# Local attention in a whole-model kernel: layer constants behind the late addition, output products apart, turned banks copied in another order

## What is computed

```python
def local_attn(x, Wqkv, Wout):          # 8 heads of 64, windows of 64 rows
    q, k, v = jnp.split(x @ Wqkv.T, 3, axis=-1)
    q, k, v = map(towin, (q, k, v))
    ke, ve = (expand(k), expand(v))      # window before, own, after
    sim = jnp.einsum('bhnid,bhnjd->bhnij', q, ke) * SCALE
    attn = jax.nn.softmax(where(valid, sim, -1e9), axis=-1)
    o = jnp.einsum('bhnij,bhnjd->bhnid', attn, ve)
    return merge_heads(o) @ Wout.T
```

## Time and profile before

| | us |
|---|---|
| median of the three runs | 2078.7 |
| lowest, highest | 2075.09, 2084.13 |
| the profiled execution | 2071.32 |
| its span | 2069.5 |

### The profile page before, as it was taken

How to read it: one execution, slowest core, us unless ns; L and a number is a source line. 1 busy time by engine, 2 the same in 40 slices (tenths; PEclk the granted TensorE clock), 3 DMA queues, 4 the chain that set the end, 5 groups by cost and what they waited for, 6 DMA issues and landing times. The chain is left out here.

```text
span 2069.5 us, 67244 instructions
## 1 busy us (share of the span) xinstructions
PE 1839.4 (89%) x27305; PEld 1286.0 (62%) x27305; DVE 1509.0 (73%) x3679; ACT 1518.7 (73%) x4403; POOL 509.2 (25%) x605
## 2 busy tenths in 40 slices
PE   3888888886899999999988995879999999997998
PEld 1444444443477777677767873537777777775786
DVE  6989999997377788877875654637667676786454
ACT  3889999995588887787754557858888888774454
POOL 2000000000144344344331100114444444433110
PEclk9989999998999999999998997989999999999999
DMA  6655555550000000000001000000000000001101
GB/s 190 151 131 122 122 130 121 124 129 1 11 18 18 23 13 23 13 23 13 23 13 42 1 1 1 1 11 13 23 21 15 23 13 23 19 17 27 48 27 37
DMA packets 72805, 91.87 MB, mean 44 GB/s; under 512 B 9913, under 2 KB 65598, under 8 KB 68702
## 3 DMA queue, kind: packets, MB, share of 16 engines
q1 hardware_dynamic: 71346, 87.14, 18.0%
q10 hardware_dynamic: 1152, 0.43, 0.1%
HBM read 39.67 MB, written 31.10 MB: 34 GB/s over the span
## 5 line engine op out<-in xcount | busy, mean ns | idle before, releaser
L448 ACT ACTIVATE r_pr<-r_dist,k_negc 128x512 f32<-128x512 f32 (+1 forms) x512 | 368.2, 836 | 17.6 <-PE r_dist L337 10.1
L1301 POOL TENSOR_TENSOR f1l_pn<-f1l_p,f1l_rs 128x512 f32<-128x512 f32 (+1 forms) x256 | 208.6, 836 | 313.1 <-DVE f1l_rs L1083 313.1
L1301 POOL TENSOR_TENSOR f2l_pn<-f2l_p,f2l_rs 128x512 f32<-128x512 f32 (+1 forms) x256 | 207.5, 831 | 301.8 <-DVE f2l_rs L1083 301.8
L996 ACT ACTIVATE f1l_p<-f1l_sm,f1l_nb 128x192 f32<-128x192 f32 x512 | 212.0, 434 | 55.7 <-DVE f1l_nb L1076 55.7
L996 ACT ACTIVATE f2l_p<-f2l_sm,f2l_nb 128x192 f32<-128x192 f32 x512 | 212.0, 434 | 45.2 <-DVE f2l_nb L1076 45.2
L351 PE MATMUL r_acc<-r_pr,r_vp 128*32 128x128 f32 (+2 forms) x3584 | 200.9, 337 | 30.7 <-DVE r_pr L537 19.2
L529 DVE SCALAR_TENSOR_TENSOR r_pr<-r_pr,k_lo,r_cap 128x512 f32<-128x512 f32 x256 | 179.9, 744 | 9.5 <-ACT r_pr L448 9.2
L537 DVE TENSOR_SCALAR r_pr<-r_pr,k_hi,k_lo 128x768 f32<-128x768 f32 x256 | 163.5, 675 | 4.6 <-ACT r_pr L448 2.6
L827 PE MATMUL f1l_pj<-f1l_xt,k_wqkv 128*128 128x512 f32 x244 | 133.4, 629 | 2.2 <-ACT f1l_qt L976 1.4
L827 PE MATMUL f2l_pj<-f2l_xt,k_wqkv 128*128 128x512 f32 x244 | 132.9, 627 | 2.4 <-ACT f2l_qt L976 1.4
L1076 DVE TENSOR_REDUCE f2l_nb<-f2l_sm 128x4 f32<-128x768 f32 x128 | 116.0, 947 | 16.8 <-PE f2l_sm L858 16.6
(11 more groups left out here) (418 smaller groups left out, 4725.2 us busy)
## 6 DMA issues: line engine op xcount, KB each, us to landing
rbf_rows<-r_part SPq DMA_DIRECT2D x112, 128.0 KB, 1.9
r_qs<-rbf_rows SPq DMA_DIRECT2D x30, 384.0 KB
r_ks<-rbf_rows SPq DMA_DIRECT2D x30, 384.0 KB
f1l_vs<-f1l_vv SPq DMA_DIRECT2D x64, 128.0 KB, 2.4
f2l_vs<-f2l_vv SPq DMA_DIRECT2D x64, 128.0 KB, 2.4
rbf_rows<-r_part SPq DMA_DIRECT2D x16, 384.0 KB, 2.6
rbf_rows<-r_part SPq DMA_DIRECT2D x16, 256.0 KB, 2.9
out<-k_x SPq DMA_DIRECT2D x16, 256.0 KB, 2.3
```

The source lines that it names most:

```text
L448: nc.scalar.activation(pr[:, n % RING, e, cols], dist[:, e, cols], ACT.Exp, scale=K["negc"][:, h:h + 1]).then_inc(done, 1)
L996: ins = nc.scalar.activation(p[:, u % 2, k, :], sm[:, u % 2, k // 2, k % 2 * PW:(k % 2 + 1) * PW], ACT.Exp, bias=nb[:, u % 2, k:k + 1], ac ...
L1301: ins = nc.gpsimd.tensor_tensor(pn[:, u % 2, at:at + HU * w].rearrange("p (k c) -> p k c", k=HU), p[:, u % 2, :, cols], r.broadcast_to([P, ...
```

## The change

On VectorE the constants move from behind `leave_turned(2t+1)` to behind `leave_values(2t-1)`; `route_shift` moves from there to behind the first `reciprocals`; and in even units the `tp` copy goes ahead of the tail's. On TensorE `turn` gets a wait for `s_ps` ahead of the transposes into `xa`; and in the 14 steps that end with `use(b+2, 0)` (`ahead`) the four output products are spread: one after the first turn, one after the second, two after the third projection. In all other steps they stay where they are.

```diff
--- before.py
+++ after.py
@@ -869,6 +869,7 @@
                 for k in range(HU):
                     nc.tensor.transpose(tp[:, k * P:(k + 1) * P], pn[:, u % 2, k * P:(k + 1) * P], K["ident"][:])
                 wait(pe, s_oe, n - n % 2)
+                wait(pe, s_ps, n)
                 for k in range(HU // 2):
                     mm = nc.tensor.transpose(xa[:, 0, XS + k * P:XS + (k + 1) * P],
                                              pn[:, u % 2, (HU + k) * P:(HU + k + 1) * P], K["ident"][:])
@@ -905,13 +906,15 @@
                                                   skip_group_check=True)
                 mm.then_inc(s_pv, 1)
 
-            def output(t, half):
-                if half == 0:
+            def output(t, chunks):
+                if t < 0:
+                    return
+                if chunks[0] == 0:
                     pe.wait_ge(s_oe, 2 * t + 2)
-                for c in (2 * half, 2 * half + 1):
+                for c in chunks:
                     mm = nc.tensor.matmul(xa[:, 1, XO:XO + P], ot[:, t % 2, c, :], K["wout_l"][:, c * P:(c + 1) * P],
                                           start=(c == 0), stop=(c == HP - 1))
-                if half == 1:
+                if chunks[-1] == HP - 1:
                     mm.then_inc(s_w, 1)
 
             for k in range(1 + 2 * HP):
@@ -928,19 +931,22 @@
             def step(t):
                 b, i = t // NT, t % NT
                 more = b + 1 < B
+                ahead = i == NT - 1 and b + 2 < B
                 if more:
                     use(b + 1, 3 * i + 1)
                 turn(2 * t)
-                if t:
-                    output(t - 1, 0)
+                output(t - 1, (0,) if ahead else (0, 1))
                 if more:
                     use(b + 1, 3 * i + 2)
-                if t:
-                    output(t - 1, 1)
+                if not ahead:
+                    output(t - 1, (2, 3))
                 turn(2 * t + 1)
+                if ahead:
+                    output(t - 1, (1,))
                 if more:
                     use(b + 1, 3 * i + 3)
-                if i == NT - 1 and b + 2 < B:
+                if ahead:
+                    output(t - 1, (2, 3))
                     use(b + 2, 0)
                 values(2 * t)
                 if t + 2 < T:
@@ -959,8 +965,7 @@
             for t in range(T):
                 step(t)
             places()
-            output(T - 1, 0)
-            output(T - 1, 1)
+            output(T - 1, (0, 1, 2, 3))
 
         @block.scalar
         def _(act):
@@ -1086,8 +1091,11 @@
                 b, par, u = place(n)
                 dve.wait_ge(s_t, n + 1)
                 wait(dve, s_pv, n - 1)
+                if u % 2 == 0:
+                    nc.vector.tensor_copy(pt[:, u % 2, 0:HU * P], tp[:]).then_inc(s_pt, 1)
                 nc.vector.tensor_copy(pt[:, u % 2, HU * P:], xa[:, 0, XS:XS + 2 * P]).then_inc(s_ps, 1)
-                nc.vector.tensor_copy(pt[:, u % 2, 0:HU * P], tp[:]).then_inc(s_pt, 1)
+                if u % 2 == 1:
+                    nc.vector.tensor_copy(pt[:, u % 2, 0:HU * P], tp[:]).then_inc(s_pt, 1)
 
             def leave_values(n):
                 b, par, u = place(n)
@@ -1250,22 +1258,6 @@
                     route_step(t - 1)
                 if t:
                     leave_values(2 * t - 1)
-                if t < NT * SEARCH:
-                    route_shift(t)
-                if finding:
-                    pick(first)
-                leave_turned(2 * t)
-                if soon:
-                    reciprocals(2 * t + 2)
-                if t:
-                    residual(t - 1)
-                if finding:
-                    pick(first + 1)
-                leave_turned(2 * t + 1)
-                if soon:
-                    reciprocals(2 * t + 3)
-                if finding:
-                    pick(first + 2)
                 k = 2 * (t - NT * ANGLES)
                 if C and NT * ANGLES <= t < NT * FRACTIONS and k < SINES:
                     constant(k)
@@ -1276,6 +1268,22 @@
                     constant(k)
                     if k + 1 < CONSTANTS:
                         constant(k + 1)
+                if finding:
+                    pick(first)
+                leave_turned(2 * t)
+                if soon:
+                    reciprocals(2 * t + 2)
+                if t < NT * SEARCH:
+                    route_shift(t)
+                if t:
+                    residual(t - 1)
+                if finding:
+                    pick(first + 1)
+                leave_turned(2 * t + 1)
+                if soon:
+                    reciprocals(2 * t + 3)
+                if finding:
+                    pick(first + 2)
                 leave_values(2 * t)
 
             for t in range(T):
```

## The result

| | before | after |
|---|---|---|
| median of six runs, us | 2077.15 | 2114.69 |
| lowest, highest | 2074.61, 2084.13 | 2107.32, 2116.55 |
| profiled execution, its span | 2071.32, 2069.5 | 2113.92, 2112.1 |

The changed kernel is slower by 1.85%: the ratio is 1.0185, 95% interval 1.0166 to 1.0203. Forecast were +29.9 us and 2108.6 us; the medians differ by 37.5 us and the two profiled spans by 42.6 us.

A forecast was written before the change was run, and what follows sets the result against it. TensorE was taken to bound the kernel, 89% busy. Terms +38.7 - 9.9 + 1.1 = +29.9 us on the profiled 2071.3 us gave 2101.2 us; plain runs lie 7.4 us higher, so 2108.6 us, range 2088 to 2123.

The forecast's parts named there:

- Part 1, the chain: Last steps of a batch: product, residual, copies and L824 become serial; L824 1.32 us later, 28 times, +38.7 us with search steps.
- The search steps: Steps 51 and 55 of each stage: `pick` between residual and copies adds an estimated 0.43 us each, 1.7 us in all.
- Part 2, the constants: First light stage, batches 4 to 9: constants moved to where POOL is idle regain most of 11.64 us, -9.9 us.
- the four steps that I had expected to stay long: Constants exceeding the room before the copy: the eight L1206 cost 0.7 us, steps 24, 36 and 38 0.2 to 0.4 each.
- Under 3 us: Sign that the forecast is right: batches 4 to 9 of the two light stages differ by less than 3 us.
- Part 3, the shift: `route_shift` behind the first reciprocal is blocked by POOL; mean 0.53 to about 1.3 us, 0.015 us in 72 steps, +1.1 us.
- The order: POOL starts 0.25 us after the first reciprocal, L1110 would start 0.26 us after it, so L1110 was taken as blocked.
- Part 4: Full copy first in even units, and TensorE's added wait for the tail's copy: cost 0, gain 0, bounds -2 and +2 us.
- The hole filled: Rival: copies of the second turn don't wait for products, the 0.42 us hole ahead of L824 goes; -21.7 us, 2057, chance 0.08.
- The boundary at a third of its cost: Rival: other PE work or a shorter chain absorbs part of the batch-end cost; +4 us, 2083 us, chance 0.06.
- constants whose excess stays: Rival: the constants' excess has another cause and stays, so the change does little; +39.8 us, 2118 us, chance 0.07.
- POOL's second instruction going first: Rival: L1110 also waits for the second of POOL's pair, another 0.57 us; +40 us more, 2149 us, chance 0.07.

The follow-up runs named there:

- constants one place ahead: Kernel before with only the constants (and the search step there) exchanged with the second reciprocal, so constants run ahead of it: 2062.01 us against 2077.95, ratio 0.9923.
- Constants alone: Kernel before with only the constants moved behind `leave_values(2t-1)`, the shift staying behind them: 2068.73 us, ratio 0.9975.
- products back: Changed kernel with the output products where they were before; constants, shift, copy order and wait stay as changed: 2072.67 us against 2077.95, ratio 0.9968.
- shift alone: Kernel before with only `route_shift` moved behind the first reciprocal: 2080.27 us, ratio 1.0034.
- residual behind with the shift moved: Changed kernel with the residual behind the second turn's copies in the spread steps and `route_shift` just ahead of the second reciprocal: 2059.42 us against 2077.95, ratio 0.9914.
- products alone: Kernel before with only the output products spread in the `ahead` steps, without the new wait: 2116.28 us against 2073.57, ratio 1.0198.
- residual behind: Changed kernel with the residual behind the copies of the second turn in the 14 steps per stage that spread the products: 2069.77 us, ratio 0.9976.
- wait in odd units: Changed kernel with TensorE's new wait for `s_ps` in odd units only: 2116.14 us against 2077.95, ratio 1.0186.

## Why the prediction was right, and where it was off

**Part 1, the chain.** Right in mechanism and size: +1.32 us forecast, +1.34 measured in the undisturbed steps, L824 1.33 us later in the rows above. The intermediate times hold too: the second turn starts 1.93 us after the first L870 (forecast 1.90), products 2 and 3 at 3.75 (3.72), the residual at 4.39 (4.37). Part of that agreement is luck. The projections were to start at 1.04 and 2.86 us and take 0.86 each; they start at 0.97 and 2.81 and take 0.96 and 0.94, and the two errors cancel. The search steps cost 1.79 us where nothing else is long, forecast 1.32 + 0.43 = 1.75. My way of watching it was wrong: I had the weight loads' wait grow from 15.4 us to about 34 us; it is 22.3 us, because the products' weight loads now stand between the projection's and the hole, and the idle time of the weight loads grows only from 1.1 to 1.6 us a step. TensorE's own wait, 3.9 to 19.6 us, is the row to watch.

**Part 2, the constants.** Forecast -9.9 us. With the same steps in the kernel without the spread, the six batches are 7.9 us shorter, and the shift's 0.2 us in their six boundary steps is in that, so about -9. Most of the four steps that I had expected to stay long did: steps 36 and 38 by 0.4 each, step 23 by 1.2 where I had 0.7, step 24 by 0.2 there and not in the changed kernel. "Under 3 us" between the stages was 1.7. That GpSimd is the cause of the excess, and not something else that stays, is shown by constants one place ahead.

**Part 3, the shift.** The size is right: about 1.3 us forecast, 1.326 measured, and the shift ends 0.275 to 0.280 us behind GpSimd's first instruction, where I had 0.28. Third steps are 0.02 us longer and the first two of a batch no longer at all, where I had 0.015 in each. The order rested on 0.01 us between two estimated starts. In the records it is the other way round: the shift starts 4 to 12 ns ahead of GpSimd's instruction in all 96 steps and is held up all the same. So starts this close don't tell who is held up, and that it came out as forecast was in part luck. As I said, the shift costs nothing in the boundary steps of the changed kernel, where the copies wait for the product anyway. Alone it costs 0.2 us in each, 7 us in all by the runs.

**Part 4** cost nothing that can be seen: TensorE's L870 waits for the copies for 1.1 and 0.5 us a stage, in the kernel before for 1.7 in each. No run has this part alone.

**What the sum lacked.** Forecast +29.9, measured +37.5 by the medians. In the two profiled executions the terms that I had come to 39.3 us in the last steps of a batch, -0.8 where those steps no longer have constants beside GpSimd, and -8.0 in all others: 30.5 us beside the 29.9. What the sum had nowhere is single long steps, so that its nearness to the medians is not all merit. Six of them are at the ends of batches 0, 5 and 10 of each stage, with 0.8 to 1.5 us more than the rest, together 6.7 us. One of them, TensorE's timeline:

```profile
591.43 0.39 PE L893 MATMUL f1l_xa<-f1l_pt,f1l_vv 64*64 64x128 f32 x7
592.80 0.48 PE L893 MATMUL f1l_xa<-f1l_pt,f1l_vv 64*64 64x128 f32 x9 [0.97 <-issue]
```

Sixteen matmuls of one line stop after seven for 0.97 us, with no semaphore in between. Stops of this kind with over 0.5 us of idle time, inside one line's matmuls of the light stages and with no semaphore, occur once in the profiled execution of the kernel before, not at a boundary, and six times in that of the changed kernel, in just these six steps. Constants alone has 0, constants one place ahead 1, products back 1, shift alone 2, residual behind with the shift moved 2, products alone 3, residual behind 3, wait in odd units 5. One execution of each is little; the cause stays open.

The seventh long step is that of batch 12 in the second stage, a search step: 12.08 us, where the same step of the first stage takes 10.49. It has no stop. TensorE's granted clock is at its 1.2 GHz level for a stretch that starts right behind the longest wait for L824, and the sixteen matmuls of L893 take 1.13 us instead of 0.67:

```profile
1843.59 0.83 PE L824 MATMUL f2l_tp<-k_ident,f2l_z 128*128 128x128 f32 x4 [1.96 <-DVE f2l_pt L1098]
1844.36 1.13 PE L893 MATMUL f2l_xa<-f2l_pt,f2l_vv 64*64 64x128 f32 x16
```

```profile
1843.50:1848.00 4.50, 4.41 (x104) 4.09 (x108) 2.07 (x6) 1.16 (x2) 1.61 (x2) 0.62 0.18 41
```

This one belongs to the change. Three kernels have this wait of 1.96 us in step 51 of each stage: the changed one, products apart alone and the wait in odd units. In each the step takes 12.1 us in one of its two stages and 10.5 in the other. The seven kernels without it have no lower clock in that step. The second search step (55) has a wait of 1.89 us and kept its clock in all six. So with the wait that the change made long goes a further 1.6 us, in half of the cases at step 51.

Other stretches at 1.2 GHz fall elsewhere in each execution. In the changed kernel the window from 679 to 684 us has a mean of 0.66, right behind a wait of TensorE of 1.96 us for L1106 beside ScalarE's sines:

```profile
679.00:684.00 5.00, 4.64 (x19) 3.48 (x20) 3.06 (x7) 3.74 (x16) 1.79 (x2) 0.66 0.00 0
```

That step took 11.82 us instead of 10.26. The version with the constants one place ahead has the same (11.93) and is quicker than the kernel before, so this is no effect of the change. Nor is the end of the program: TensorE's last 350 or so matmuls take 53.7 us at a mean clock of 0.85 instead of 49.5 at 0.93, which is the 4.2 us behind the second stage, and constants one place ahead also has its last 17.5 us at the lower clock.

**The rivals.** The hole filled: it needed one more link taken out, and then came true in part (8.32 us a step, 0.17 of the 0.42 us). The boundary at a third of its cost, and constants whose excess stays, are ruled out by the 1.34 us a step and by the 9.5 us that the constants give one place ahead. POOL's second instruction going first did not occur in any of 96 shifts (1321 to 1330 ns).

## What to carry to other kernels

Before moving a product to fill a hole, look up who waits for its result and what stands behind that reader in the reader's own queue: if the hole's own releaser is there, the hole grows. When tiny VectorE operations last about as long as GpSimd's, look at what releases GpSimd, and run them ahead of that release; one place was worth 9.5 us in the trace here, and 0.8% (0.5 to 1.0) by the runs. And cost every part alone: a part can be free only because another part is late at the same place. The shift was such a part: 7 us alone, nothing in the boundary steps of the changed kernel.

## What the runs showed of the hardware that was not expected

- A VectorE instruction held up by GpSimd goes between two GpSimd instructions that stand in line: the shift took 1321 to 1330 ns in all 96 cases, and GpSimd's pair of instructions took 1.79 us there instead of 1.61. The Trainium skill (SBUF — State Buffer, Who interferes with whom) tells of the exclusive lock; the traces agree with it, in that the shift ends 0.28 us behind GpSimd's first instruction each time.
- A start 0.05 us behind GpSimd's is enough to be held up: in the kernel before, a TENSOR_TENSOR of 128x1 (L1176) that started so took 1.00 us, while its like (L1157) that started 1 ns behind took 0.16 us. But it is not needed: the shift is held up though its record starts 4 to 12 ns ahead. In the traces of the earlier trace rows and of constants one place ahead, the same 128x32 instruction has 0.91 and 0.25 us.
- TensorE's granted clock can fall to its 1.2 GHz level right behind a single wait of 1.96 us: it did so in three of the six steps 51 that have this wait, and in none of the six steps 55, which have 1.89 us.
- TensorE can stop for about 1 us in the middle of one line's matmuls, at places that move when instructions are added or taken away. Whether late loading of instructions does this stays open.
